# One wait on the transfer queue and 18 unread transposes at the beginning of an attention stage

## Chip, cores and metric

One core of a Trainium2 chip runs the whole program in one launch. The metric is the device time in microseconds (us), the median of several runs. Every position below is in us from the start of the profiled span.

## What is computed

Layer norm, an attention with one matrix per head, and a feed-forward part with block-wise quantized operands, each with a residual. The change touches only the attention, cut here to what matters:

```python
# x: (16, 512, 256) float32, H = 16 heads of D = 16
x_h = x.reshape(b, t, h, d).transpose(0, 2, 1, 3)          # of the layer-normed x
xw  = jnp.einsum('bhtd,hde->bhte', x_h, w_att_val)         # "q" in the kernel
att = jnp.einsum('bhte,bhse->bhts', xw, x_h) / jnp.sqrt(d)
att = jax.nn.softmax(att, axis=-1)                         # needs each row's maximum
o   = jnp.einsum('bhts,bhsd->bhtd', att, vx)
x = x + (o @ out_w.T + out_b);  x = x + ffn(layernorm(x))
```

## The kernel before, in words

The 16 batches are worked one after the other, and in each the 16 heads in four "quads" of four heads. A quad has four steps (j = 0 to 3), one for each 128 keys. The scores are made twice. First TensorE makes a "maximum tile" (128 queries by 512 keys, L929) for each head and each 128 queries, 16 tiles to a quad, and VectorE reduces each to its row maxima (L1199, semaphore `m_used`). Then, per step, TensorE makes the scores again with keys as rows (L937), adds the negated maxima by a second matmul (L940), ScalarE takes the exponential (L1081), and TensorE weighs the values (L962). The maximum tiles run nearly two quads ahead, through a ring of four PSUM banks, so TensorE waits for VectorE where the ring is full.

What a quad's tiles read are its "stacks" in SBUF: `x_stack` (two transfers of 256 KB, L162) and `q_stack` (four of 128 KB, L172), loaded from DRAM. The maxima of a quad travel: GpSimd splits them (L694, L697), VectorE turns them (L1208), ScalarE's queue stores them to DRAM (L1158, 16 KB, semaphore `max_stored`) and loads them back in another layout (L1168, two of 8 KB, semaphore `max_loaded`), and only then the quad's step scores can be made.

The attention block begins so. Before batch 0's steps, TensorE makes 28 maximum tiles: 16 of quad 0, then 12 of quad 1 (a loop over n = 0 to 13, two tiles at each n, so n = 8 to 13 are quad 1's). Then it waits for quad 0's maxima and makes step 0's scores. The first maximum tiles in batch 0's step 0 are quad 1's last four; the first of step 1 are quad 2's first, and they wait for quad 2's stacks. I number the steps through: step 4 is quad 1's first, step 9 is quad 2's second, and its first maximum tiles read batch 1's quad 0 stacks.

SyncE's queue goes in a fixed order: quad 1's `x_stack`, batch 0's second half of the stores, quad 2's stacks, a wait for quad 0's maxima to be loaded (`max_loaded[0]`), quad 3's stacks, 12 transfers that copy the feed-forward weights inside DRAM, a wait for all of them, one weight load (L839), then batch 1's stores (L199) and its quad 0 stacks. ScalarE's queue: quad 1's `q_stack`, store and load of quad 0's maxima, then batch 2's x (512 KB, L1172).

```python
for n in range(FIRST_MAXIMA // ROWS):          # 14 times; PAIRS * TT is 8
    ...
    max_scores(-1, g, at)
pe.wait_ge(pool_set, POOL_SET)
step_scores(0, 0, 0, True)                     # waits for max_loaded[0] first
```

The block ahead of this one already has such unread transposes (`warm(FILL)`, 50 of them, L337), made while the first input is awaited.

Of the kernel before, what the change touches and what calls it, by code (L numbers as in the profile page):

```python
# [10 lines left out]
P = 128  # L11
# [3 lines left out]
TT = T // P  # L15
# [3 lines left out]
QUAD = 4  # L19
QUADS = H // QUAD  # L20
PAIRS = 2
# [32 lines left out]
def wait(eng, semaphore, count):  # L54

    if not (isinstance(count, int) and count <= 0):
        eng.wait_ge(semaphore, count)
# [94 lines left out]
def row_tile(tile, m):  # L152

    return tile[KM * m:KM * m + KM, :, :]


def load_x_stack(queue, b, g, x_stack, x_rows, stack_loaded):
    a = g * QUAD // HH
    for m in range(ROWS):
        h = g * QUAD % HH + PAIRS * m  # L160
        src = x_rows[bass.ds(b, 1), a, :, :, h:h + PAIRS, :]
        queue.dma_start(row_tile(x_stack[g], m).bitcast(F32),  # L162
                        src.rearrange("o k d h t -> (o k d) h t")).then_inc(stack_loaded[g], 16)


def load_q_stack(queue, b, g, q_stack, q_rows, stack_loaded):
    a = g * QUAD // HH
    for m in range(ROWS):
        h = g * QUAD % HH + PAIRS * m
        src = q_rows[bass.ds(b, 1), a, :, :, h:h + PAIRS, :]  # L170
        for k in range(2):
            queue.dma_start(row_tile(q_stack[g], m)[2 * D * k:2 * D * k + 2 * D, :, :].bitcast(F32),  # L172
                            src.rearrange("o k d h t -> (o k d) h t")).then_inc(stack_loaded[g], 16)


def load_stacks(sp, b, g, x_stack, q_stack, x_rows, q_rows, stored, stack_loaded):
    sp.wait_ge(stored[g * QUAD // HH], STORES * (b + 1))
    load_x_stack(sp, b, g, x_stack, x_rows, stack_loaded)
    load_q_stack(sp, b, g, q_stack, q_rows, stack_loaded)
# [17 lines left out]
def store_parts(sp, b, a, dst, parts, stored):  # L197
    for k, t in enumerate(parts):
        sp.dma_start(dst[bass.ds(b, 1), a, k].rearrange("o d h t -> (o d h) t"), t[:, a, :].bitcast(F32))\  # L199
          .then_inc(stored[a], 16)  # L200
# [234 lines left out]
def attention_block(nc, ctx, x, max_rows, w_gate, w_up, w_down, slabs, slabs_kept, first_x,  # L435
# [6 lines left out]
    def pb(name, shape):  # L442
        return ctx.enter_context(nc.psum_tensor(name, shape, F32))

    def sem(name):
        return ctx.enter_context(nc.semaphore(name))
# [19 lines left out]
    scores = [pb(f"scores{k}", [P, T]) for k in range(QUAD)]  # L466
# [13 lines left out]
    bias_added, max_stored = sem("bias_added"), sem("max_stored")  # L480
    m_ready, m_used, m_split, m_low, m_turned = (
        sem(n) for n in ("m_ready", "m_used", "m_split", "m_low", "m_turned"))
# [44 lines left out]
    def max_bank(b, g, n):  # L527

        q, k = aimed(g, n, QUAD * TT)
        if isinstance(b, int) and QUADS * b + q == 0:  # L530
            return (*ring, *scores)[k % 8]
        return bank(("max", g, n))

    def aimed(g, n, per):

        quads, number = divmod(2 * per + n - BEHIND * per // (QUAD * TT), per)
        return g + quads, number
# [56 lines left out]
    def room(tiles, b):  # L594

        counts, sample = {}, {}
        for tile in tiles:
            n, c, probe = AT[tile], b, b if isinstance(b, int) else 2
            while True:
                n -= len(ring)  # L600
                if n < 0:
                    n, c, probe = n + len(TILES_IN_RING), c - 1, probe - 1
                if isinstance(b, int) and c < -1:
                    break
                if in_ring(TILES_IN_RING[n], c):
                    semaphore, count = emptied(TILES_IN_RING[n], c)
                    size = emptied(TILES_IN_RING[n], probe)[1]
                    if semaphore not in counts or size > sample[semaphore]:
                        counts[semaphore], sample[semaphore] = count, size
                    break  # L610
        return list(counts.items())
# [34 lines left out]

    AHEAD = 6
    FIRST_MAXIMA = 2 * QUAD * TT - BEHIND
    ZEROED = 2
    POOL_SET = ZEROED + 3 + ROWS + 2 * QUADS  # L650
    COPIES = 12
# [5 lines left out]
    with nc.Block() as block:  # L657
# [146 lines left out]
        def _(sp):  # L804
# [72 lines left out]
            load_x_stack(sp, 0, 1, x_stack, x_rows, stack_loaded)  # L877
            store_parts(sp, 0, 1, x_rows, (xh, xl, xl, xh), stored)
            store_parts(sp, 0, 1, q_rows, (qh, ql), stored)
            load_stacks(sp, 0, 2, x_stack, q_stack, x_rows, q_rows, stored, stack_loaded)  # L880
            sp.wait_ge(max_loaded[0], 16 * ROWS)
            load_stacks(sp, 0, 3, x_stack, q_stack, x_rows, q_rows, stored, stack_loaded)
# [18 lines left out]
            for k, (_, width) in enumerate(FK):  # L901
                sp.dma_start(down_T[k][P - width:P, :].rearrange("p (n c) -> p n c", c=P), down_kept[k, 0:width])\
                  .then_inc(ffn_loaded, 16)
# [2 lines left out]

        @block.tensor
        def _(pe):
            def max_scores(b, g, n):

                q, at = aimed(g, n, PAIRS * TT)
                c, q = b + q // QUADS, q % QUADS
                p, s = divmod(at, TT)
                tiles = [("max", g, ROWS * n + m) for m in range(ROWS)]
                if isinstance(c, int) and c == 0 and q == 0 and p == 0:
                    if s == 0:
                        pe.wait_ge(first_loaded, STACK)
                elif isinstance(c, int) and c == 0 and q == 0:
                    if s == 0:
                        pe.wait_ge(stack_loaded[0], STACK)  # L920
                elif at == 0:
                    pe.wait_ge(stack_loaded[q], STACK * (c + 1))
                if isinstance(c, int) and c == 0 and q == 0:
                    wait(pe, m_used, ROWS * (at - 4) + ROWS)
                else:
                    for semaphore, count in room(tiles, b):
                        pe.wait_ge(semaphore, count)
                for m in range(ROWS):
                    pe.matmul(max_bank(b, g, ROWS * n + m)[:, :], row_tile(q_stack[q], m)[:, p, s * P:(s + 1) * P],  # L929
                              row_tile(x_stack[q], m)[:, p, :], start=True, stop=True).then_inc(m_ready, 1)  # L930
# [12 lines left out]
            def step_scores(b, g, j, start):  # L943
                if j == 0:
                    pe.wait_ge(max_loaded[g], 16 * ROWS * (b + 1))
                for p in range(PAIRS):
                    key_scores(QUADS * b + g, g, j, p, start)
# [105 lines left out]
                    quad(b, g, isinstance(b, int) and b == 0, isinstance(b, int) and b == B - 1)  # L1053

            for n in range(FIRST_MAXIMA // ROWS):
                if n == PAIRS * TT + AHEAD:
                    pe.wait_ge(pool_set, POOL_SET)
                    step_scores(0, 0, 0, True)
                g, at = divmod(PAIRS * TT * QUADS - FIRST_MAXIMA // ROWS + n, PAIRS * TT)
                max_scores(-1, g, at)  # L1060
            if AHEAD == FIRST_MAXIMA // ROWS - PAIRS * TT:
                pe.wait_ge(pool_set, POOL_SET)
# [10 lines left out]
        def _(act):  # L1073
# [87 lines left out]
            def load_maxima(i, g):  # L1161

                act.wait_ge(max_stored, 16 * (i + 1))
                if isinstance(i, int) and i < 2:
                    act.wait_ge(pool_set, ZEROED)
                rows = max_rows[bass.ds(i, 1)].rearrange("o (l h s) r t -> (o l) h (s r t)", l=2, h=QUAD)
# [25 lines left out]
        def _(dve):  # L1192
            def reduce_max(b, g, k):
                q, number = aimed(g, k, QUAD * TT)
                n, m = divmod(number, ROWS)
                p, s = divmod(n, TT)
                at = TT * (PAIRS * m + p) + s
                dve.wait_ge(m_ready, QUAD * TT * (QUADS * b + q) + number + 1)
                dve.tensor_reduce(neg_max[q % 2][:, at:at + 1], max_bank(b, g, k)[:, :],  # L1199
                                  AX.X, ALU.max, negate=True).then_inc(m_used, 1)  # L1200
# [3 lines left out]
            def turn_maxima(i, g, start):  # L1204
                dve.wait_ge(m_low, i + 1)
                if not start:
                    dve.wait_ge(max_stored, 16 * (i - 1))
                dve.transpose(max_turned[g % 2][:, :], max_cols[g % 2][:, :]).then_inc(m_turned, 1)  # L1208
# [111 lines left out]
            def batch(b):  # L1320
                for g in range(QUADS):
                    quad(b, g, isinstance(b, int) and b == 0, isinstance(b, int) and b == B - 1)

            for k in range(FIRST_MAXIMA):
                if k == QUAD * TT:
                    turn_maxima(0, 0, True)
                reduce_max(-1, *divmod(QUADS * QUAD * TT - FIRST_MAXIMA + k, QUAD * TT))
            batch(0)
# [488 lines left out]
```

## Time and profile before

| | us |
|---|---|
| median of 3 runs | 1459.87 |
| the three runs | 1459.37, 1459.87, 1463.14 |
| the profiled execution's own time | 1459.96 |
| its span, first to last instruction | 1458.0 |
| TensorE busy | 1421.5 (97%) |
| VectorE busy | 1264.2 (87%) |
| ScalarE busy | 866.0 (59%) |
| GpSimd busy | 659.2 (45%) |

The span is cut in 40 slices on the profile's page; TensorE is at nine tenths or more in all of them but the first two and the last. The attention ends after about 24 slices, the rest is the feed-forward part. 2.0 us lie outside the span, and the profiled execution is within 0.1 us of the median.

### The profile page before, as it was taken

The page shows a single profiled execution, that of the slowest core. Times are in us where ns is not written, and L with a number is a line of the kernel's source. Part 1 is how long each engine was busy: PE and PEld are TensorE (multiplying, and loading weights), DVE is VectorE, ACT ScalarE, POOL GpSimd, SP SyncE. Part 2 cuts the span into 40 slices and gives each one's busy share as a digit, 9 for nine tenths or more (in the row PEclk, how much of TensorE's full clock was granted, in tenths as well). Part 3 has the DMA queues.
Part 4 walks back from the last instruction along what each step waited for, and adds up shares of the span by engine and source line. Part 5 has one row for each costly group of instructions (what it writes and reads, how often), then busy time and mean ns, then how long its engine had stood idle before and what let it go on. Part 6 is the DMA issues. An engine that isn't in the chain of part 4 may idle for free. (4 is left out here: it accounts for less than half of the span.)

```text
span 1458.0 us, 32405 instructions
## 1 busy us (share of the span) xinstructions
PE 1421.5 (97%) x8612; PEld 892.2 (61%) x8612; DVE 1264.2 (87%) x2652; ACT 866.0 (59%) x1731; POOL 659.2 (45%) x911
## 2 busy tenths in 40 slices
PE   6899999999999999999999998999999999999999
PEld 4445555555555555555555554577777777777776
DVE  6788888888888888888888887699999999999996
ACT  1577777777777777777777777443333333343333
POOL 3455545545545545546546522234343343434341
PEclk8799999999999999999999999999999999999999
DMA  6856456455456455465455451000000000000000
GB/s 204 235 147 186 123 146 189 123 149 184 122 155 180 123 156 176 127 157 173 131 157 154 133 155 46 1 18 15 14 18 14 18 14 18 14 17 15 14 19 22
DMA packets 99785, 148.09 MB, mean 102 GB/s; under 512 B 21024, under 2 KB 58272, under 8 KB 99744
## 3 DMA queue, kind: packets, MB, share of 16 engines
q1 hardware_dynamic: 82672, 137.22, 32.9%
q10 hardware_dynamic: 17072, 10.37, 2.7%
q8 instruction: 21, 0.34, 0.1%
q14 instruction: 20, 0.16, 0.0%
HBM read 85.02 MB, written 65.27 MB: 103 GB/s over the span
## 5 line engine op out<-in xcount | busy, mean ns | idle before, releaser
L1199 DVE TENSOR_REDUCE neg_max<-ring 128x1 f32<-128x512 f32 x1016 | 636.0, 681 | 82.0 <-PE ring L929 81.7
L1081 ACT ACTIVATE probs<-scores 128x512 f32<-128x512 f32 x1024 | 534.3, 604 | 171.0 <-PE scores L940 165.7
L1714 PE MATMUL gu_bank<-splits,f_x_T 128*128 128x352 f32 x1024 | 313.7, 459 | 0.1
L929 PE MATMUL ring<-x_stack,q_stack 64*128 64x512 f32 x1016 | 230.7, 450 | 20.5 <-DVE neg_max L1199 11.4
L1714 PEld LDWEIGHTS gu_bank<-splits,f_x_T 128*128 128x128 f32 x1024 | 189.6, 190 | 95.4 <-ACT f_x_T L1688 0.5
L962 PE MATMUL ring<-probs,v_quad 128*32 128x512 f32 x2048 | 246.4, 599 | 0.2
L937 PE MATMUL scores<-q_stack,x_stack 64*128 64x512 f32 x1024 | 206.7, 397 | 2.7 <-DMA max_stack<-max_rows 1.5
L940 PE MATMUL scores<-max_stack,max_ones 64*128 64x512 f32 x1024 | 204.2, 392 | 0.0
L929 PEld LDWEIGHTS ring<-x_stack,q_stack 64*128 64x128 f32 x1016 | 98.0, 187 | 172.7 <-DVE neg_max L1199 114.5
L1404 POOL TENSOR_TENSOR f_small<-f_small,eps 128x1 f32<-128x1 f32 x64 | 42.9, 671 | 296.0 <-DVE f_small L1371 296.0
L1673 ACT ACTIVATE h_T<-h_bank 128x256 f32<-128x256 f32 (+1 forms) x128 | 56.0, 488 | 169.9 <-PE h_bank L1728 169.9
L1736 PE MATMUL y_bank<-splits,h_T 128*128 128x256 f32 x640 | 148.9, 380 | 0.6 <-ACT h_T L1673 0.6
L962 PEld LDWEIGHTS ring<-probs,v_quad 128*32 128x32 f32 x2048 | 53.9, 109 | 124.4 <-issue 73.0
L1736 PEld LDWEIGHTS y_bank<-splits,h_T 128*128 128x128 f32 x640 | 116.7, 190 | 14.4 <-DVE x_all L1589 0.8
L694 POOL TENSOR_TENSOR max_cols<-neg_max,one 128x16 fp32r<-128x16 f32 x64 | 13.8, 216 | 216.9 <-DVE neg_max L1199 216.9
L937 PEld LDWEIGHTS scores<-q_stack,x_stack 64*128 64x128 f32 x1024 | 98.5, 186 | 20.6 <-ACT probs L1081 7.3
L940 PEld LDWEIGHTS scores<-max_stack,max_ones 64*128 64x128 f32 x1024 | 98.5, 186 | 19.6
L1455 POOL TENSOR_TENSOR hq<-h_level,h_scale 128x704 f32<-128x704 f32 x63 | 87.3, 1386 | 24.4 <-DVE h_level L1448 24.4
L717 POOL TENSOR_TENSOR pv_rows<-pv_more,pv_rows 128x512 f32<-128x512 f32 x63 | 80.9, 1284 | 31.6 <-ACT pv_more L1087 31.5
L1688 ACT ACTIVATE f_x_T<-x_bank 128x256 f32<-128x256 f32 x64 | 24.5, 383 | 117.8 <-PE x_bank L1702 117.8
L709 POOL TENSOR_TENSOR x_all<-x_all,out_bias 128x256 f32 (+1 forms) x64 | 47.0, 735 | 102.9 <-DVE x_all L1267 102.6
L1442 DVE SCALAR_TENSOR_TENSOR h_level<-h_mag,h_units 128x704 f32<-128x704 f32 x63 | 56.2, 892 | 39.4 <-ACT h_mag L1437 39.4
(144 smaller groups left out, 2015.5 us busy)
## 6 DMA issues: line engine op xcount, KB each, us to landing
x_rows<-splits SPq DMA_DIRECT2D x128, 256.0 KB, 3.8
x_stack<-x_rows SPq DMA_DIRECT2D x126, 256.0 KB, 4.0
q_stack<-q_rows SPq DMA_DIRECT2D x248, 128.0 KB, 4.0
q_rows<-splits SPq DMA_DIRECT2D x64, 256.0 KB, 2.2
out_dram<-x_all SPq DMA_DIRECT2D x64, 128.0 KB, 1.7
x_all<-in_L_attn_x_dram ACTq DMA_DIRECT2D x14, 512.0 KB, 4.2
w_raw<-slabs SPq DMA_DIRECT2D x14, 192.0 KB, 3.9
slabs_kept<-w_turned SPq DMA_DIRECT2D x14, 192.0 KB, 5.3
```

Source lines behind the costliest of these rows:

```text
L717: pool.tensor_tensor(pv_rows[g % 2][:, :], pv_more[:, :], pv_rows[g % 2][:, :], ALU.add)\
L929: pe.matmul(max_bank(b, g, ROWS * n + m)[:, :], row_tile(q_stack[q], m)[:, p, s * P:(s + 1) * P], row_tile(x_stack[q], m)[:, p, :], start= ...
L937: pe.matmul(scores[ROWS * p + m][:, :], row_tile(x_stack[g], m)[:, p, j * P:(j + 1) * P], row_tile(q_stack[g], m)[:, p, :], start=True, st ...
L940: pe.matmul(scores[ROWS * p + m][:, :], row_tile(max_ones, m)[:, 0, :], row_tile(max_stack[g % 2], m)[:, p, :], start=False, stop=True).th ...
L962: m = pe.matmul(bank(tile)[VW * h:VW * h + VW, :], v[q][:, j, h, :], probs[j][:, k, :], start=(j == steps[0]), stop=(j == steps[1]))
L1081: act.activation(probs[j][:, k, :], scores[k][:, :], ACT.Exp).then_inc(p_ready, 1)
L1199: dve.tensor_reduce(neg_max[q % 2][:, at:at + 1], max_bank(b, g, k)[:, :], AX.X, ALU.max, negate=True).then_inc(m_used, 1)
L1442: dve.scalar_tensor_tensor(out=level, in0=mag, scalar=SHIFT_MIN, in1=units, op0=ALU.max, op1=ALU.subtract)\
L1455: pool.tensor_tensor(blocks(out), blocks(level), spread(scale, BLK), ALU.mult).then_inc(done, 1)
L1673: act.activation(h_T[1 - u][:, first:end, :], h_bank[k][:, 0:end - first, :], ACT.Copy).then_inc(h_moved, 1)
L1714: m = pe.matmul(gu_bank[c][:, :], x_T[u][:, a, :], gate_up_T[:, a, c * CH:(c + 1) * CH], start=(a == 0), stop=(a == HALVES - 1))
L1736: m = pe.matmul(y_bank[:, :], h_T[u][:, k, :], down_T[k][:, :], start=(k == 0), stop=(k == len(SLICES) - 1))
```

## The change

SyncE waits, before it issues quad 2's stacks, until the store of quad 0's maxima has landed. And TensorE makes 8 transposes of the identity ahead of n = 10 and 10 ahead of n = 12, into a bank of the step scores that nothing reads before it is overwritten; they wait for all 16 tiles of quad 0 to be reduced, since these had used that bank.

```diff
+    FILL = {2: 8, 4: 10}
...
             store_parts(sp, 0, 1, q_rows, (qh, ql), stored)
+            sp.wait_ge(max_stored, 16)
             load_stacks(sp, 0, 2, x_stack, q_stack, x_rows, q_rows, stored, stack_loaded)
             sp.wait_ge(max_loaded[0], 16 * ROWS)
...
+            def warm(n):
+
+                for _ in range(n):
+                    pe.transpose(scores[QUAD - 1][:, 0:P], ident[:, :], ident[:, :])
...
             for n in range(FIRST_MAXIMA // ROWS):
+                if n - PAIRS * TT in FILL:
+                    pe.wait_ge(m_used, QUAD * TT)
+                    warm(FILL[n - PAIRS * TT])
```

## Rows read from the trace of the kernel before

**Rows 1.** The page: the span, and busy time of each engine.
```profile
span 1458.0 us, 32405 instructions
...
PE 1421.5 (97%) x8612; PEld 892.2 (61%) x8612; DVE 1264.2 (87%) x2652; ACT 866.0 (59%) x1731; POOL 659.2 (45%) x911
```

**Rows 2.** TensorE by stretch: length, busy (matmuls), granted clock (1 is full), DMA share, GB/s.
```profile
1.58:5.90 4.32, 4.32 (x20) 1.00 0.61 183
6.10:9.30 3.20, 3.20 (x30) 1.00 0.79 203
18.30:22.55 4.25, 0.00 (x0) 1.00 0.76 201
...
23.00:24.40 1.40, 1.32 (x8) 0.51 0.95 212
45.76:49.73 3.97, 3.97 (x16) 0.50 1.09 300
...
50.51:53.70 3.19, 3.19 (x16) 0.50 1.12 306
```

**Rows 3.** Timeline of TensorE: start, length, instruction, count, idle before and its releaser.
```profile
35.51 1.39 PE L929 MATMUL ring<-x_stack,q_stack 64*128 64x512 f32 x4 [1.88 <-DVE neg_max L1199]
38.28 1.39 PE L929 MATMUL ring<-x_stack,q_stack 64*128 64x512 f32 x4 [1.38 <-DVE neg_max L1199]
41.22 0.80 PE L937 MATMUL scores<-q_stack,x_stack 64*128 64x512 f32 x2 [1.55 <-DMA max_stack<-max_rows]
...
43.06 1.08 PE L929 MATMUL ring<-x_stack,q_stack 64*128 64x512 f32 x4
45.76 0.80 PE L929 MATMUL ring<-x_stack,q_stack 64*128 64x512 f32 x2 [1.61 <-DVE neg_max L1199]
...
50.51 0.80 PE L929 MATMUL ring<-x_stack,q_stack 64*128 64x512 f32 x2 [0.78 <-ACT raw_x L1115]
...
55.38 0.50 PE L929 MATMUL ring<-x_stack,q_stack 64*128 64x512 f32 x2
...
65.37 0.49 PE L929 MATMUL ring<-x_stack,q_stack 64*128 64x512 f32 x2
...
75.75 0.51 PE L929 MATMUL ring<-x_stack,q_stack 64*128 64x512 f32 x2
```

**Rows 4.** Timeline of ScalarE's queue at the attention's beginning.
```profile
33.72 1.14 ACTq L1158 DMA_DIRECT2D max_rows<-max_turned  x1
37.70 0.54 ACTq L1168 DMA_DIRECT2D max_stack<-max_rows  x2
38.27 0.43 ACTq L1172 DMA_DIRECT2D x_all<-in_L_attn_x_dram  x1
```

**Rows 5.** Timeline of SyncE's queue: start, length of issuing, transfers.
```profile
33.59 1.41 SPq L162 DMA_DIRECT2D x_stack<-x_rows  x2
35.03 1.97 SPq L172 DMA_DIRECT2D q_stack<-q_rows  x4
41.10 1.11 SPq L162 DMA_DIRECT2D x_stack<-x_rows  x2
...
56.14 0.40 SPq L839 DMA_DIRECT2D w_raw<-slabs  x1
...
64.66 1.74 SPq L172 DMA_DIRECT2D q_stack<-q_rows  x4
```

**Rows 6.** Timeline of VectorE: the reductions of n = 12 and 13.
```profile
39.11 2.48 DVE L1199 TENSOR_REDUCE neg_max<-ring 128x1 f32<-128x512 f32 x4 [0.29 <-PE ring L929]
```

**Rows 7.** All engines by stretch: busy times, granted clock, DMA share, GB/s.
```profile
33.60:35.00 1.40, 0.03 (x2) 0.00 (x0) 1.40 (x4) 0.00 (x0) 0.86 (x2) 0.50 0.02 6
...
41.70:42.50 0.80, 0.80 (x6) 0.67 (x5) 0.00 (x0) 0.05 (x1) 0.00 (x0) 0.50 0.17 46
```

**Rows 8.** DMA issues of 0 to 3 us: KB each, median us to landing.
```profile
qw<-in_L_attn_w_att_val_dram ACTq DMA_DIRECT2D x3, 2.0 KB, 2.8
```

**Rows 9.** DMA issues of 20 to 24 us, where three kinds of transfer overlap.
```profile
x_rows<-splits SPq DMA_DIRECT2D x3, 256.0 KB, 7.2
```

**Rows 10.** DMA issues of 36.5 to 37 us: quad 2's last q_stack transfers.
```profile
q_stack<-q_rows SPq DMA_DIRECT2D x2, 128.0 KB, 4.2
```

## The prediction

> **What bounds the kernel now.** I read the page first: TensorE is busy 97% of the span and VectorE 87% [rows 1]. With so full a TensorE, whatever shifts the first steps forward shifts the end by as much, unless something later holds it back. Next the stretches and the timeline of the beginning. There TensorE isn't full, and until 53.7 us it runs at the lower of its two clock levels, 1.2 in place of 2.4 GHz (0.50 in the column) [rows 2]. Around the edit the reader should see three waits: 1.88 us ahead of n = 10 and 1.38 us ahead of n = 12, both for VectorE's reductions, and 1.55 us ahead of step 0's scores at 41.22, for quad 0's maxima [rows 3]. That last one is the end of a chain in ScalarE's queue: stored from 33.72, landed by 37.70 when the load is issued, loaded by about 41.1, where SyncE, which waits for the same, resumes [rows 4, 5]. So the store takes 3.98 us and the load 3.35 to 3.4. While the store was issued SyncE was issuing quad 2's stacks too, from 33.59 to 37.00 [rows 5].
>
> After step 0 the starts of the steps are 41.22 (step 0's scores), 45.76, 50.51, 55.38, and 65.37 for step 6 [rows 3]. Steps 1 and 2 take 4.75 and 4.87 us at the low clock; steps 3 to 5 take (65.37 - 55.38) / 3 = 3.33 us at the full one.
>
> **The turns, what they cost.** The 50 turns of the block before are the same instruction. 20 of them took 4.32 us, 216 ns each; then 30 took 3.20 us, 107 ns each [rows 2]. (The column says 1.00 in both stretches, but the rate doubles at 6 us; it has nothing to report before its first event.) That is the two levels, and TensorE had done nothing but such turns when it rose. At 216 ns, 8 turns are 1.73 us and fit in the 1.88 us wait. 10 turns are 2.16 us against 1.38: they push n = 12 from 38.28 to about 38.75, since the last pair of n = 11 stops streaming some 0.8 us after the group's start at 35.51 plus 0.2. n = 13 follows at 39.2 and TensorE is free at 39.6, still ahead of the maxima. VectorE's four reductions, 0.62 us each, shift by the same 0.47, from 39.11 to 39.58, and end at 42.06 [rows 6]. If the clock is up already these turns are 1.07 us and push nothing. The wait on `m_used` is met at about 32.8, before TensorE comes to it. So the turns cost nothing by themselves, 0.5 us if the maxima came far earlier than I think.
>
> **What the turns may give.** With them TensorE is busy from about 33.4 to 35.1 and, almost without a gap, from 35.5 to 39.6, and goes on with step 0 from 40 to 42. Without them its longest busy stretch before the rise, 3.97 us from 45.76, wasn't enough (the clock stays at 0.50), and it rose in the stretch that began at 50.51, after a pause of 0.78 us [rows 2]. At the start of the kernel it rose after about 4.4 us of turns. I expect the rise between 36.5 and 43. Then steps 1 and 2 run at 3.33 us each: (55.38 - 45.76) - 2 x 3.33 = 9.62 - 6.66 = **3.0 us** gained. Bounds: 0 if it doesn't rise, 3.0 if it is up before step 1.
>
> The Trainium skill (TensorE: Matmul & The Clock Gate, Part 4: PE-mode transpose) says that transposes don't count as busy for the clock gate. By that the 18 turns give nothing and the sum lacks the 3.0. Here the trace speaks against it: the rate doubled amid 50 turns with nothing else on the engine [rows 2].
>
> **The store and the load of the maxima.** Without SyncE's transfers beside it the store meets an idle DMA: its share is 0.02 from 33.6 to 35.0 as it is [rows 7]. Nothing in the trace shows this store alone. Above, it is bounded by today's 3.98 us; below by the nearest small transfer with little beside it, 2.8 us for 2 KB [rows 8]. I take 2.8, since it would be alone: landed at 36.5, 1.2 earlier. The load then starts together with the stacks of quad 2, as it ran beside them before: 3.4 us again (bounds 2.8 to 4.0), loaded at 39.9. Step 0's scores start at 39.95, 1.3 earlier.
>
> **Quad 2's stacks.** They are moved from 33.59 to 36.5, past the store. SyncE issues two x_stack and four q_stack transfers, 3.4 us [rows 5], so the last is issued 2.9 us later, at about 39.4. Before, the last landed at 36.6 + 4.2 = 40.8 [rows 10], which step 1 (45.76) never felt. Now 40.8 + 2.9 = 43.7. But batch 2's x, 512 KB on the other queue, now starts at 37.1 instead of 38.27 [rows 4] and runs through the middle of them, which adds up to 1 us; I take 0.5, so 44.2. On the other side step 1's first tiles wait until step 0's third tile is reduced: VectorE is free at 42.06, and three reductions end at 43.9 with the clock up; with the clock low step 0's tiles start at 39.95 + 1.84 = 41.8 in place of 43.06 and the reduction ends at 44.4. Either way **step 1 starts at 44.2 to 44.4 in place of 45.76: 1.5 us gained** (bounds: 2.3 with no late stack; below 0 if the stacks land after 45.76).
>
> Behind them on SyncE: quad 3's stacks wait for the maxima to be loaded, so they go at 39.9 in place of 41.10, and the 12 copies follow 1.2 earlier. The queue isn't late, but the transfers themselves are: DMA is nearly full from 35 to 55 apart from the hole of 0.8 us at 41.7 [rows 7], and its work begins 2.9 us later and gets back that hole only. So the wait for the copies, which ended at 56.14 [rows 5], ends some 1.9 us later, and batch 1's quad 0 stacks with it: issued from 64.66 to 66.4, landed at about 69.6, with the 1.9 at 71.5. Step 9 needs them, at 75.75 before [rows 3], at 71.25 after a gain of 4.5. A stall of 0.25: I take **0.3 us given back** (bounds 0 to 1.5, for the maxima of quad 1 are loaded in the same crowd and may be late for step 4 too).
>
> **Sum.** 1.5 + 3.0 - 0.3 = 4.2 us. The profiled execution's 1459.96 becomes 1455.8; the median lies 0.1 lower: 1455.7 us.
>
> **Rivals.** First, *the clock doesn't rise, or falls back at once.* For it: a busy stretch of 3.97 us did not raise it [rows 2], the turns are not all back to back, and after step 0 TensorE waits up to 2 us for stacks and reductions. Against it: 4.25 us of idleness passed before it was down at 23.0 [rows 2], and the turns raised it once. What is left is the earlier maxima: 1.5 - 0.1 = 1.4, so 1458.5 us. By the skill's sentence above it would come to this.
>
> Second, *the wait doesn't quicken the store* (the change doesn't do what it says): the 3.98 us are the store's own. Then step 0 stays at 41.2, quad 2's stacks start at 37.7, 4.1 later, and land at 44.9 to 45.9, so step 1 is at about 45.4. TensorE then has its wait of 1.5 us ahead of step 0, and the clock rises late or not: 0.4 gained, 1459.5 us. With the clock up it would be 3.0 better, 1456.5.
>
> Third, the other side: *quad 2's stacks take the place of the wait.* Where transfers of this size overlapped on both queues, they took up to 7.2 us [rows 9]. From 39.4 that is 46.6 for step 1, and with the low clock kept, as TensorE would idle for 4 us, everything after it is 0.9 later, and step 9's stacks with it: 1461.2 us. It decides from the point where the stacks land after 45.76, with the clock low; with the clock up it must be after 48.8. Against it: the 4.2 of the same transfers at a full DMA [rows 10].
>
> **How the numbers follow.** The likeliest, at 0.62, is the sum: 1455.7, its own range 1454.3 to 1457.3 (no late stack; twice 0.8 given back). No clock: 0.22. Store not quicker: 0.08. Stacks late: 0.08. 0.3% is 4.4 us, about what a measurement of this kernel can tell from no change. The sum lies just on the near side of that. I give half of the likeliest case and a little to faster, where the stack and step 9 cost nothing (0.34); slower by over 0.3% is the far end of the late stacks and whatever else the later transfers hold back (0.06); within, 0.60. The range runs from 1454.0 (all waits hidden) to 1459.6 (the second rival), which leaves out under 2 in 10.
>
> **What would show it.** In the profile after: turns at about 33.4 and 36.6, 216 ns apart; the granted clock at 1.00 by 43 us and kept; the load of the maxima issued at about 36.5; step 0's scores at about 40; step 1 at 44.2, ahead of it a wait for q_stack or for a reduction; then steps 3.3 us apart, step 3 at about 51; step 9 at 71.5 with a small wait for q_stack. It is wrong if the clock is at 0.50 in steps 1 and 2, if the load is still issued near 37.7, or if step 1 comes after 45.

## The result, and the profile after

| | before | changed |
|---|---|---|
| median of 22 executions each, us | 1460.38 | 1462.97 |
| profiled execution, us | 1459.96 | 1463.86 |
| its span | 1458.0 | 1460.3 |

The ratio of the changed kernel to the one before is 1.0015, with a 95% interval of 1.0010 to 1.0021: 2.2 us slower, inside the 0.3% that I called "within", but clear of noise and on the other side of my forecast of 1455.7. The medians themselves lie 2.6 us apart, and 1462.97 is above the end of my range, 1459.6. Three single executions far off all others (2862 us of the turns alone, 1802 and 2056 us of the kernel with the copies moved) are in none of the ratios and medians below.

First what the three parts did, in the order of the prediction. TensorE's timeline, the changed kernel (start, length, instruction, count, idle before and its releaser):

```profile
33.47 1.97 PE L915 MATMUL scores<-ident 128*128 128x128 f32 x8
35.42 1.39 PE L937 MATMUL ring<-x_stack,q_stack 64*128 64x512 f32 x4
36.74 1.43 PE L915 MATMUL scores<-ident 128*128 128x128 f32 x10
38.19 1.10 PE L937 MATMUL ring<-x_stack,q_stack 64*128 64x512 f32 x4
39.43 0.50 PE L945 MATMUL scores<-q_stack,x_stack 64*128 64x512 f32 x2
...
41.26 0.73 PE L937 MATMUL ring<-x_stack,q_stack 64*128 64x512 f32 x4 [0.64 <-DVE neg_max L1210]
45.41 0.80 PE L937 MATMUL ring<-x_stack,q_stack 64*128 64x512 f32 x2 [3.42 <-DMA q_stack<-q_rows]
...
50.16 0.80 PE L937 MATMUL ring<-x_stack,q_stack 64*128 64x512 f32 x2 [0.78 <-ACT raw_x L1126]
...
55.38 0.50 PE L937 MATMUL ring<-x_stack,q_stack 64*128 64x512 f32 x2
...
72.36 0.50 PE L937 MATMUL ring<-x_stack,q_stack 64*128 64x512 f32 x2
74.19 0.50 PE L945 MATMUL scores<-q_stack,x_stack 64*128 64x512 f32 x2 [1.32 <-DMA max_stack<-max_rows]
...
77.41 0.51 PE L937 MATMUL ring<-x_stack,q_stack 64*128 64x512 f32 x2
```

Against [rows 3]: step 0's scores come at 39.43 in place of 41.22, 1.8 us sooner. Step 1 comes at 45.41 in place of 45.76, and ahead of it is a new wait of 3.42 us for quad 2's stacks. Step 3 starts at 55.38, the same hundredth as before: of the gain nothing is left. Step 8 begins at 72.36 against 72.31, and its scores wait for their maxima, so step 9 begins at 77.41 in place of 75.75. That 1.66 us is what the rest of the kernel is late by (1.2 to 1.7 up to the last batch); a further 0.7 us comes in the attention's last quads, where most of the traces below, the one with SyncE's queue untouched and no turns among them, lose 0.5 to 1.2 us against the one trace of before, so I don't count it to the change.

The granted clock over the same time, by half microseconds (busy matmuls, clock, DMA share, GB/s):

```profile
36.50:37.00 0.50, 0.50 (x3) 0.50 0.37 41
37.00:37.50 0.50, 0.50 (x6) 0.96 0.79 147
...
43.00:43.50 0.50, 0.00 (x0) 1.00 1.09 246
43.50:44.00 0.50, 0.00 (x0) 0.86 1.00 221
44.00:44.50 0.50, 0.00 (x0) 0.50 1.05 238
...
53.50:54.00 0.50, 0.50 (x8) 0.50 1.18 341
54.00:54.50 0.50, 0.50 (x12) 0.90 1.01 290
```

The turns did raise the clock, to 2.4 GHz at 37.0 us, in the middle of the second lot. In all 14 profiles of kernels with the 18 turns it rose between 35.7 and 39.0; in the three without them (before, and the runs "wait only" and "kernel before with the later x" below) at 53.7, 54.6 and 49.8. It fell back at 43.9, in the wait ahead of step 1, and rose again only at 54.1, against 53.7 before. Steps 1 and 2, which were to gain 3.0 us from it, ran at 1.2 GHz once more.

ScalarE's queue and SyncE's queue, two views of the changed kernel:

```profile
33.63 1.14 ACTq L1169 DMA_DIRECT2D max_rows<-max_turned  x1
35.72 0.54 ACTq L1179 DMA_DIRECT2D max_stack<-max_rows  x2
36.29 0.47 ACTq L1183 DMA_DIRECT2D x_all<-in_L_attn_x_dram  x1
...
69.00 0.56 ACTq L1179 DMA_DIRECT2D max_stack<-max_rows  x2
```

```profile
35.71 1.11 SPq L162 DMA_DIRECT2D x_stack<-x_rows  x2
36.87 1.98 SPq L172 DMA_DIRECT2D q_stack<-q_rows  x4
...
44.55 4.59 SPq L860 DMA_DIRECT2D slabs<-in_L_ffn_w_up_dram  x1
...
58.00 0.40 SPq L841 DMA_DIRECT2D w_raw<-slabs  x1
58.44 2.17 SPq L199 DMA_DIRECT2D x_rows<-splits  x4
65.44 0.81 SPq L199 DMA_DIRECT2D q_rows<-splits  x2
66.29 1.28 SPq L162 DMA_DIRECT2D x_stack<-x_rows  x2
68.41 1.74 SPq L172 DMA_DIRECT2D q_stack<-q_rows  x4
```

The store landed 2.07 us after its issue instead of 3.98 [rows 4], so alone it is even quicker than my lower bound of 2.8. It took 2.07 to 2.09 in every profile with the wait; in the seven without it 2.08 to 4.45, so the 3.98 of the one trace of before is near the long end, and the wait is worth 0 to 2.4 us there. Quad 2's stacks start at 35.71, 2.1 us later than before and 0.8 sooner than I had it. Yet the last of them lets step 1 go only at 45.4. Behind them SyncE's chain is late as worked out: the wait for the copies ends at 58.00 against 56.14 [rows 5], 1.9 later. (The place varies: 56.0 to 57.7 in the profiles without the wait in which nothing else was put ahead of step 0 and the copies were left alone, 58.0 to 58.8 in all with it.) Then it grows: batch 1's quad 0 `q_stack` goes at 68.41 against 64.66. Its transfers now run beside the load of quad 2's maxima, issued at 69.00: from there to step 8's scores it takes 5.2 us, where the kernel before had at most 72.65 - 69.28 = 3.4, for there the scores didn't wait. The last of these stacks landed at 76.05, in place of 70.03; that is later than the 75.75 at which step 9 had begun before.

### The profile page after: what moved, and what is told of

Its sections match the earlier page's. It is cut to its first block and busy times, and to the rows that moved or that the text cites. A ratio compares the mean times of both kernels' runs of the same rounds, so it can differ in the third digit from the quotient of the medians.

```text
span 1460.3 us, 32442 instructions
## 1 busy us (share of the span) xinstructions
PE 1424.1 (98%) x8630; PEld 895.6 (61%) x8630; DVE 1264.0 (87%) x2652; ACT 866.1 (59%) x1731; POOL 659.1 (45%) x911
```

## The experiments

My theory after this (A): SyncE's wait is the loss, by the late stacks and what comes behind; the turns are free. The rivals: the turns cost; batch 2's x is what delays the stacks; the clock isn't worth anything here. All ratios are to the kernel before, run beside it on the same chip. The mean clock is that of each execution's whole span. Kernels that leave out or move something still compute all of the reference.

**Wait only.** The change without the 18 turns.

```diff
-                if n - PAIRS * TT in FILL:
-                    pe.wait_ge(m_used, QUAD * TT)
-                    warm(FILL[n - PAIRS * TT])
```

> The wait of SyncE stays, the 18 turns are gone. Theory A (the moved stacks of quad 2 are the loss; the turns cost nothing, and what they give is thrown away when TensorE idles ahead of step 1): as the changed kernel, 0.1 to 0.2% over the kernel before, with step 0's scores at about 39.5, step 1 at about 45.4 behind a wait for q_stack, and step 8 waiting over 1 us for its maxima; the clock is at 0.50 until about 54. Rival B (the turns are the loss, or push what follows them): within 0.05% of the kernel before, or faster, since the store of the maxima is 2 us shorter.

Ratio 1.0008 (0.9999 to 1.0017). Step 0's scores at 40.1, then a wait of 2.47 us for `q_stack`, step 1 at 45.68, the clock low until 54.6. Step 8 did not wait for its maxima in this execution, so that part of the expectation failed. The wait alone makes the stacks late (the last landed at 45.6), but whether it loses time by itself stays within the noise.

**Turns only.** The change without SyncE's wait.

```diff
-            sp.wait_ge(max_stored, 16)
```

> The 18 turns stay, SyncE's wait is gone, so quad 2's stacks go at 33.6 as before. Theory A: the clock rises at about 37 and is kept, since TensorE's longest pause is then about 2 us ahead of step 0 at 41.2; step 0's tiles are ready sooner, step 1 starts at about 44.8, steps 1 and 2 run at 3.3 us each, step 3 is at about 51.5 and step 8 at most 0.5 us late: 3 to 4 us faster than the kernel before (ratio 0.9973 to 0.9980). Rival B: the turns give nothing or cost: ratio 1.000 to 1.002, with the clock at 0.50 in steps 1 and 2 or a late step somewhere after.

Ratio 1.0000 (0.9992 to 1.0009), so the 3 to 4 us were missed, though the first part of the expectation came true. TensorE's timeline shows both halves:

```profile
44.69 0.50 PE L936 MATMUL ring<-x_stack,q_stack 64*128 64x512 f32 x2 [2.61 <-DMA q_stack<-q_rows]
...
47.89 0.50 PE L936 MATMUL ring<-x_stack,q_stack 64*128 64x512 f32 x2 [0.95 <-ACT raw_x L1125]
...
51.34 0.51 PE L936 MATMUL ring<-x_stack,q_stack 64*128 64x512 f32 x2
...
75.77 0.50 PE L936 MATMUL ring<-x_stack,q_stack 64*128 64x512 f32 x2 [3.03 <-DMA q_stack<-q_rows]
```

The clock was kept, steps 1 and 2 took 3.2 and 3.45 us, and step 3 began at 51.34, 4.0 ahead of the kernel before. Step 9 then waited until 75.77 for batch 1's quad 0 stacks, and gave all of it back. The wait cost more than its length, as the clock fell behind it (0.59 and 0.50 in the two microseconds from 77): step 9 took 4.5 us, where the kernel before had 3.2. The issues of that time (KB each, us to landing), from the stretches 66.2 to 66.5 and 67.5 to 67.8:

```profile
x_all<-in_L_attn_x_dram ACTq DMA_DIRECT2D x1, 512.0 KB, 9.2
...
q_stack<-q_rows SPq DMA_DIRECT2D x1, 128.0 KB, 8.3
```

In this profile the store of the maxima took 2.08 us even without SyncE's wait, as SyncE came to quad 2's stacks only at 34.34. So step 0 came at 40.20, and batch 2's x, issued at 36.38, ran through quad 2's stacks as it does in the changed kernel. The last `q_stack` took 8.3 us, where the kernel before had 4.1. As the steps are early, so is ScalarE's queue, and it issues batch 3's x at 66.2, right into these stacks; before, it went at 69.9, when they had nearly landed.

**Batch 2's x after step 0's exponentials**, the rest as changed.

```diff
             load_maxima(0, 0)
-            load_x(2)
...
+                    if first and g == 0 and j == 0:
+                        load_x(2)
```

> The changed kernel, but ScalarE's queue loads batch 2's x (512 KB) after step 0's exponentials, at about 42, not right behind the maxima at 36.3. Theory A1 (batch 2's x, interleaved with quad 2's stacks, takes about 1.5 us of their time): quad 2's stacks land at about 43.5 to 44, the wait ahead of step 1 shrinks from 3.4 to under 2 us, and the clock may survive it; then 2 to 4 us faster than the changed kernel. Rival A2 (the stacks are late by their own start alone): step 1 still at 45 to 45.5, the clock falls, same time as the changed kernel.

Ratio 1.0016 (1.0007 to 1.0024). Here step 1 didn't wait for stacks at all. Its line, and then quad 2's four `q_stack` transfers in this run (37.6 to 39.3) and in the changed kernel (36.8 to 38.5), KB each and median us to landing:

```profile
44.73 0.57 PE L937 MATMUL ring<-x_stack,q_stack 64*128 64x512 f32 x2 [1.83 <-DVE neg_max L1211]
...
q_stack<-q_rows SPq DMA_DIRECT2D x4, 128.0 KB, 4.0
...
q_stack<-q_rows SPq DMA_DIRECT2D x4, 128.0 KB, 6.7
```

The x cost each of them 2.7 us. Without it the last one took 4.2 from issue, about the 4.2 of [rows 10], and landed 6.9 us after SyncE began the stacks at 36.53; in the changed kernel it was 9.7 (35.71 to 45.37). Step 1 then came when VectorE had reduced, some 1.5 us sooner than in the changed kernel if both are counted from the attention's first tiles (33.06 here, 32.24 there). So theory A1 was right on the stacks, with too small a price. The clock still fell, at 45.0, with no wait of TensorE since its rise longer than 1.83 us, and was back at 48.4. Step 3 began at 52.70, 2.7 us ahead of the kernel before; but step 9 waited 2.91 us for `q_stack` and began at 76.91, 1.2 behind. The end is the same: what step 1 to 3 gain is lost at step 9.

**24 more turns ahead of step 1**, the rest as changed.

```diff
+                    if start and j == 1:
+                        pe.wait_ge(p_ready, QUAD)
+                        warm(HOLD)
```

> The changed kernel with 24 more unread turns between step 0's and step 1's maximum tiles (2.6 us at the full clock), where TensorE waits for quad 2's stacks. Theory A: the clock stays at 1.00, steps 1 and 2 take 3.3 us each instead of 4.75 and 5.2, step 3 is at about 52 in place of 55.4; what follows is then held by the late transfers (step 4's or step 8's maxima, step 9's stacks), so of the 3.3 us some 1 to 2 are lost again: 1 to 3 us faster than the changed kernel. Rival B (the clock isn't worth anything here, since ScalarE, VectorE or the transfers hold steps 1 and 2): within 0.5 us of the changed kernel.

Ratio 1.0009 (1.0000 to 1.0018), against 1.0016 for the run before it and 1.0015 for the changed kernel. The profile has step 3 at 52.9, 2.5 us ahead, and the clock at 1.00 throughout. Step 9 comes at 74.8 after a wait of 1.23 us for `q_stack`, 0.95 ahead of the kernel before, and the span is that kernel's, 1458.0. So rival B is out, steps 1 and 2 do run faster; but of its 2.5 us 1.5 are lost by step 9, and against the changed kernel the gain of 0.06% is within the noise.

**Batch 3's x four steps later**, with three kernels: the turns alone, the kernel before, and the changed one with the 24 turns.

```diff
-                    if (g, j) == (1, 2) and prepared(b + 3):
+                    if (g, j) == ((2, 2) if isinstance(b, int) and b == 0 else (1, 2)) and prepared(b + 3):
```

> The 18 turns without SyncE's wait, and batch 0 loads batch 3's x (512 KB) at step 10 instead of step 6. Theory C (the 3 to 4 us that the clock gives at steps 1 and 2 are lost at step 9, since batch 1's quad 0 stacks are the bound there, and batch 3's x runs through them: the last of them took 8.3 us from issue in place of 4.1): step 9 starts near 73, not at 76.1, keeps the full clock, and 2.5 to 3.5 us of the gain reach the end: ratio 0.9975 to 0.9985. Rival D (the stacks are late by SyncE's chain of stores and copies alone, whatever runs beside them): step 9 still after 75, ratio 0.9995 to 1.001.

> The kernel before, with batch 3's x loaded at step 10 as in the run above, as its control. Theory C: before, the x started after batch 1's quad 0 stacks had landed, so there is nothing to gain: within 0.05% of the kernel before, step 9 at 76.1. If this alone is faster by over 0.1%, the gain of the run above isn't that of the turns.

> The changed kernel with the 24 turns ahead of step 1 and batch 3's x at step 10. Theory C: step 1 waits for quad 2's stacks as long as before this edit (the wait of SyncE is in it), the clock is kept, steps 1 to 8 are 2 to 2.5 us ahead of the kernel before, and step 9 waits at most 0.5 us: ratio 0.998 to 0.9990. Rival D: step 9 at 75 or later, ratio 1.000 to 1.001.

Turns alone: 0.9999 (0.9990 to 1.0008). The kernel before: 0.9996 (0.9987 to 1.0005). Changed with 24 turns: 0.9990 (0.9981 to 0.9999), where the same without the later x had 1.0009. The control shows that the x alone brings nothing that can be told. In the profile of the first, step 9 begins at 71.5 with no wait for stacks and the span is 1453.9, 4.1 under the kernel before. But its 11 executions fall into two groups: five with a mean clock of 0.994 or 0.995 and spans of 1453.9 to 1456.3, six with 0.989 to 0.992 and 1457.6 to 1460.0. In the third kernel all 11 have 0.994 or more and lie within 1455.3 to 1457.2. So the 18 turns alone raise and keep the clock in part of the executions only. Two profiles show it directly, this one and that of the next run, whose kernel is the same up to SyncE's weight copies at 44.4; both waited 1.5 us ahead of step 0 and 1.81 ahead of step 1:

```profile
44.25 0.50 PE L936 MATMUL ring<-x_stack,q_stack 64*128 64x512 f32 x2 [1.81 <-DVE neg_max L1209]
...
44.80 0.52 PE L946 MATMUL ring<-x_stack,q_stack 64*128 64x512 f32 x2 [1.81 <-DVE neg_max L1219]
```

In the first the clock stayed at 1.00 to the end, in the second it was at 0.50 from 45.2 to 48.6. The kernel before varies by itself too: of its 127 executions in the four groups of runs, 55 have a mean clock of at most 0.989 and a mean span of 1459.3, 66 have 0.991 to 0.993 and 1457.9. Its one trace in [rows 2] (0.989) is of the kind where the clock comes late; in the control's it was up at 49.8 and step 3 began at 54.27.

**Ten of the twelve weight copies after batch 1's x1 stores**, on top of the first of these three (diff shortened).

```diff
-            copy_weights()
-            sp.wait_ge(w_copied, 16 * COPIES)
+            copy_weights(False)
+            sp.wait_ge(w_copied, 16 * HALVES)
...
+                                store(b + 1, 1, x_rows, "x1", (xh, xl, xl, xh))
+                                copy_weights(True)
```

> As the first of this call, and of the 12 weight copies only the two that batch 0 reads go at the old place; the other ten (2.4 MB) follow batch 1's x1 stores, at about 75 us. Theory E (the copies fill the DMA from 42 to 57 and hold batch 1's stores, the loads of the maxima and so step 9): batch 1's x0 stores go at about 52 instead of 58, its quad 0 stacks land before 68, step 9 doesn't wait, and step 9 is at about 72: ratio 0.9970 to 0.9980, unless the copies cost as much where they are now (a late step 13 to 17). Rival (only the x of batch 3 mattered): the same as the first of this call.

Ratio 1.0023 (1.0012 to 1.0034). Batch 1's x0 stores went at 51.6 and its stacks at 59.5, and step 9 was on time, but the ten copies from 73.2 on did there what they had done before: the maxima of step 16 came 1.68 us late, the clock fell behind that wait (0.50 from 99.8 to 103.2), and step 17 was 1.7 us behind the kernel before. Behind the copies the stacks went at 88.97, and the store of these maxima beside them took 5.1 us; in the first run they went at 84.22, and it took 3.2. Moving the DMA work moved the late load.

**The clock held throughout.** 10 turns ahead of step 0's scores and 16 ahead of step 1 besides the 18, batch 3's x at step 10; without SyncE's wait, with it, and without it but with the x at its old place.

```diff
+                warm(FIRST)                      # FIRST = 10
                 pe.wait_ge(pool_set, POOL_SET)
                 step_scores(0, 0, 0, True)
```

> No wait on SyncE; the 18 turns and 10 more ahead of step 0's scores and 16 ahead of step 1, so that TensorE is never long idle between n = 8 and step 1; batch 3's x at step 10. Theory F (the 18 turns raise the clock, but in only part of the executions keep it to step 1; with 18 turns and the x later, five of eleven executions had a mean clock of 0.994 or more and spans of 1453.9 to 1456.3, the others 0.989 to 0.992 and 1457.6 to 1460.0): now every execution has 0.994 or more and a span of 1453.5 to 1456; ratio 0.9970 to 0.9980. Rival G (the spread of the executions has nothing to do with the clock): spans spread from 1454 to 1460 as before, ratio about 0.9990.

> The same as the first of this call, with SyncE's wait for the store of the maxima. Theory A (the wait alone, the clock held equal, costs what the later transfers of quad 2 cost): step 1 starts 0.5 to 1.5 us later than without the wait, though step 0 starts over 1 us earlier, and SyncE's chain is up to 2 us later: 1 to 2.5 us slower than the first (ratio 0.9980 to 0.9992). Rival H (the wait costs only by letting the clock fall): within 0.5 us of the first.

> The same as the first of this call, but batch 3's x at step 6 as it was. Theory C: steps 1 to 8 as in the first, then a wait of 1 to 4 us at step 9 for batch 1's quad 0 stacks; of the 4 us gained 1.5 to 3 are lost, ratio 0.9982 to 0.9995. Rival: as the first, ratio 0.9970 to 0.9980, the late x being of no use once the clock is held.

| | ratio | interval |
|---|---|---|
| held, no wait, x later | 0.9983 | 0.9974 to 0.9992 |
| held, wait, x later | 0.9981 | 0.9972 to 0.9990 |
| held, no wait, x at its old place | 0.9996 | 0.9987 to 1.0005 |

All 22 executions of the first two have a mean clock of 0.994 or 0.995, against 0.988 to 0.993 for the kernel before beside them: theory F holds for the clock, but the spans (1455.0 to 1458.7) and the ratio are less good than it said. Theory A fell here. With the clock held and the x out of the way, SyncE's wait costs nothing that can be told; what step 1 loses by it (nothing: 46.0 against 47.3 for the scores, as step 0 is 1.5 sooner) isn't a loss at all. Even so the profile of the first lost its gain: 2.3 us ahead at step 7, it waited 1.58 us for the maxima of step 8 and was 0.1 behind at step 9; it is the slowest of its eleven executions. The x costs 0.13% once the steps are early (the intervals just overlap): TensorE's timeline of the third has

```profile
76.81 0.69 PE L938 MATMUL ring<-x_stack,q_stack 64*128 64x512 f32 x2 [2.44 <-DMA q_stack<-q_rows]
```

**Four on one chip, for what was open.** The changed kernel again; the changed kernel with only the x of batch 3 later; wait and held clock with the x at its old place; wait, held clock and late x, with 8 turns ahead of step 1 in place of 16.

```diff
-    HOLD = 16
+    HOLD = 8
```

> The changed kernel once more, beside the next three on one chip: ratio 1.0010 to 1.0020, mean clock of the executions 0.990 to 0.994. It is the measure for the other three; a ratio under 1.0005 would say that the loss itself is a matter of the chip.

> The changed kernel with nothing but batch 3's x at step 10. Theory J (what makes the changed kernel slower than the one before is that its later transfers meet batch 3's x at steps 6 to 9): step 8 no longer waits over 1 us for its maxima, ratio 0.9990 to 1.0003, 0.12 to 0.25% under the changed kernel. Rival K (the lateness of SyncE's chain is enough by itself): step 8's wait stays at over 1 us and the ratio over 1.0010.

> The wait, the 18 turns and the 10 and 16 more, batch 3's x at step 6 as it was. Theory J: as the clock is held, steps 1 to 7 are 1.5 to 3 us ahead of the kernel before, and a wait at steps 8 or 9 takes 1.5 to 3 us of that: ratio 0.9995 to 1.0012. Rival: the ratio is 0.9978 to 0.9988, as with the x at step 10, and the x only mattered without SyncE's wait.

> The wait, the 18 turns and 10 more ahead of step 0, but 8 in place of 16 ahead of step 1, batch 3's x at step 10. In the run with 16 these began at 43.6, when step 0's exponentials were done, and pushed step 1 to 46.0, while quad 2's stacks can land at 44.5 to 45.5. If the turns are the limit there, step 1 starts 0.5 to 0.9 us sooner and the ratio is 0.9975 to 0.9982; if the stacks are, it is the same as with 16 (0.9981) within 0.0004. If 8 are too few, some executions have a mean clock under 0.993 and their spans are over 1457.5.

| | ratio | interval | mean clock |
|---|---|---|---|
| changed, again | 1.0013 | 1.0004 to 1.0022 | 0.991 to 0.993 |
| changed, x later | 1.0012 | 1.0003 to 1.0021 | 0.989 to 0.993 |
| wait, held, old x | 1.0013 | 1.0003 to 1.0022 | 0.992 to 0.995 |
| wait, held, x later, 8 turns | 0.9994 | 0.9984 to 1.0003 | 0.993 to 0.995 |

The first three are alike, and the fourth lies below them: with SyncE's wait, neither the held clock alone nor the later x alone takes the loss away, only the two together. So theory J fell for the changed kernel, and its forecast for the third came about (a wait of 1.51 us at step 9; step 7 had been 2.6 us ahead, step 9 was 0.05). Rival K came true in the ratio only: in the second kernel's profile step 8 waited 0.49 us, not over 1, and the time was lost elsewhere, 1.1 us by step 3 (the clock was low until 55.6), 0.8 at step 8 and 2.8 in the last batch. So what keeps that kernel slow isn't shown. This time the profile of the changed kernel had the clock back at 49.3 and began step 3 at 53.79, 1.6 us ahead, and lost that and 0.7 more by step 9, again to a transfer:

```profile
53.79 0.50 PE L937 MATMUL ring<-x_stack,q_stack 64*128 64x512 f32 x2
...
71.43 0.50 PE L945 MATMUL scores<-q_stack,x_stack 64*128 64x512 f32 x2 [0.20 <-DMA max_stack<-max_rows]
76.46 0.50 PE L937 MATMUL ring<-x_stack,q_stack 64*128 64x512 f32 x2 [1.74 <-DMA q_stack<-q_rows]
```

The third and the fourth are 0.19% apart. Two edits lie between them, the x's place and 16 or 8 turns; that the number of turns doesn't matter is likely from the fourth's median span, 1456.6, the same as with 16 on another chip. But its ratio isn't the 0.9981 within 0.0004 that I expected, and its interval holds 1. Its step 1 did come sooner, at 45.44 behind 0.67 us of waiting for the stacks, in place of 45.70.

## Why the prediction was wrong

*Turns cost nothing, 216 ns each at the low clock:* right. The first eight end at 35.44, n = 10 starts at 35.42 in the pattern of before, and the clock rose during the second lot, so they pushed nothing.

*The clock rises between 36.5 and 43:* right, at 37.0 in the profile. The Trainium skill's sentence on transposes (TensorE: Matmul & The Clock Gate, Part 4: PE-mode transpose) is contradicted again, now in this place: in 14 profiles with the turns the clock rose at 35.7 to 39.0, in the three without them not before 49.8. *That it stays up* I had taken for granted. The Trainium skill (TensorE: Matmul & The Clock Gate, HAM oscillation — how this bites in real kernels) says that a wait on a transfer can throttle TensorE again, and here the trace agrees: 3.42 us without a matmul, and the clock fell in it. The runs show that it takes less: it fell with no wait over 1.83 us (batch 2's x later), and was kept through one of 2.61 us (turns only).

*Store 2.8, load 3.4:* the store was mis-sized to the careful side, 2.07 us; the load took about 3.6. Step 0 was 1.8 us sooner, not 1.3.

*"Either way step 1 starts at 44.2 to 44.4":* this is **the first step that failed**. I shifted the stacks' landing by their later start, which was right, and took 0.5 us for batch 2's x, the wrong size: the x takes 2.7, as its own run showed. Then 38.42 (the last issue) + 4.2 + 2.7 = 45.3, and they landed at 45.37. In microseconds this is a gain of 0.35 instead of 1.5. With it went **the 3.0 us of the clock**, which I had hung on its rising alone and not on its being kept until step 1: in the profile steps 1 and 2 ran at 0.50 and gained nothing; in a second profile the clock came back at 49.3, and 1.6 us were gained by step 3. I had the idleness of up to 2 us in the first rival ("falls back at once", 0.22), and priced it at 1458.5.

*"I take 0.3 us given back":* **the second step that failed, and the one that would have failed the forecast by itself**. The shift of the copies by 1.9 us came out (measured 1.86), in part by luck, as the same wait ended anywhere from 56.0 to 57.7 without the change. The stacks' landing before, which I put at 69.6, was 70.03. But the store of batch 1's x0, whose last part took 5.5 us to land in place of 3.6, made 3.75 of it, and the late transfers then met quad 2's maxima. I looked at the stacks of step 9 and the maxima of step 4, not at the maxima of step 8, and I left out that batch 3's x is issued earlier when the steps are, into batch 1's stacks. I gave the whole term a bound of 1.5. It was 1.66 us in the profile, at a time when nothing was gained to pay for it; and where something was gained, between step 7 and step 10 it took 5.2 us from the turns alone, 1.6 from the changed kernel with the 24 turns, and 2.6 from the one with the wait and the clock held (counted at the exponentials).

*The end:* 0.35 at step 1, 0.0 at step 3, -1.66 at step 9. Shown by runs: with the turns, 1.0000 without the wait (0.9992 to 1.0009) and 1.0015 with it (1.0010 to 1.0021), so with them the wait costs; without the turns its 1.0008 is within the noise of both. That no gain arrives is shown by the four on one chip and by the held kernels: with the clock held and batch 3's x later it is 0.9981 to 0.9994 with the wait and 0.9983 without; with the x at its old place 1.0013 and 0.9996, though the clock is held. So the turns don't pay in the kernel as changed for two reasons, each enough: the clock falls in many executions, and where it doesn't, the transfers up to step 9 take the gain back. That TensorE's 97% makes every early gain reach the end was too simple. In the kernel before, batch 1's stacks landed at 70.03, 5.7 us ahead of step 9, and steps 3 to 4 us earlier looked safe; but the earlier steps moved batch 3's x into them, and they landed at 75.73 (turns only). By which of its transfers the wait makes the changed kernel slower than the one before, and not equal to it, is argued from single profiles and not shown.

Left open: how the 2.2 us divide between stacks and maxima over many executions, as only one execution of each kernel is profiled and the place of the loss moved from step 8 to step 9 between two of them; and why the time outside the span is 3.56 us in the changed kernel's profiled execution, 2.3 in the median, and 2.0 before.

The version to keep is the one with the clock held and batch 3's x at step 10, with or without SyncE's wait: 0.9981 and 0.9983 of the kernel before on one chip, 0.9990 and 0.9994 for its near relatives with the wait on two others, and medians of 1458.4 to 1458.7 us in all four. That is a gain of 1 to 3 us; only the last interval (0.9984 to 1.0003) reaches 1.

## What to carry to other kernels

A gain from a raised clock can be lost at the next wait, in some executions and not in others: list the idle time between the rise and the work that is to profit, and ask of each transfer there what happens if it is a microsecond late. When an early stage is shortened, its queues issue sooner too; a large transfer that used to go after the urgent ones may land in their midst, so check for each later load its slack and its neighbours. A wait that gives one small transfer a free DMA moves all work behind it, and in a full stretch that work can come back as a late load somewhere else. And read from the trace what released a step before its start is taken for a transfer's landing: in one run here it was VectorE, and the transfers had been there for 1.3 us.

## What was unexpected of the hardware

- A store of 16 KB with the DMA otherwise idle landed 2.07 us after issue; beside 1 MB of stacks it had taken 3.98.
- 128 KB took 4.1 us to land with no large transfer on the other queue until they had nearly landed, and 8.3 us when 512 KB had been issued on another queue about 1.2 us before; those 512 KB took 9.2 in place of 4.7.
- One transfer's issue on SyncE took 4.59 us in place of 1.07 (L860 here, L858 before), with the DMA's share at 1.0 or more in both. In all ten profiles with SyncE's wait it took 3.67 to 4.67; in the six without it that have this transfer at this place, 0.87 to 1.39 and once 2.96. All that is behind it on the queue waits; what it waited for, the profile doesn't show.
- The same 18 turns kept the clock up in five executions of eleven and not in six, by their mean clocks, and in one of two profiles with the same waits; with turns in every wait it was up in all.
